# An attention, recurrence and feed-forward block with its attention rewritten on products of weights, in finer units woven into the recurrence

## What is computed

```
q, k, v = y @ Wq, y @ Wk, y @ Wv                       # 16 heads of 64
dots = q k^T * SCALE                                    # per sequence and head
pos  = (q . rel_emb[clip(i - j, -64, 64) + 64]) * SCALE
out  = softmax(dots + pos) @ v;  x = x + out @ Wo + bo
...
def step(h, xs):                                        # 256 times, in order
    z  = sigmoid(xzt + h @ U_z + vz)
    r  = sigmoid(xrt + h @ U_r + vr)
    hh = tanh(xht + r * h @ U + vh)
    return (1 - z) * h + z * hh
...
sel = argmax(h @ gate_w.T);  g = h w_gate[sel].T;  u = h w_up[sel].T   # scaled by sigmoid(top)
x = x + (u * silu(g)) @ w_down[sel].T
```

## Time and profile before

| | |
|---|---|
| median of 3 runs | 716.01 us (714.69 to 716.34) |
| span of the profiled execution, first to last instruction | 712.3 us |
| median less span | 3.7 us |
| PE busy | 623.2 us, 87% of the span |
| DVE, ACT, POOL busy | 461.2, 323.5, 177.9 us |
| keys, queries, values | 15.4 to 60.5 us |
| forty units ahead of the recurrence | to about 150 us |
| first and last `g` of the recurrence | 161.4 and 697.7 us |

### The profile page before, as it was taken

How to read it: one execution, slowest core, us unless ns; L and a number is a source line. 1 busy time by engine, 2 the same in 40 slices (tenths; PEclk the granted TensorE clock), 3 DMA queues, 4 the chain that set the end, 5 groups by cost and what they waited for, 6 DMA issues and landing times.

```text
span 712.3 us, 26221 instructions
## 1 busy us (share of the span) xinstructions
PE 623.2 (87%) x7909; PEld 511.6 (72%) x7909; DVE 461.2 (65%) x3362; ACT 323.5 (45%) x1253; POOL 177.9 (25%) x789
## 2 busy tenths in 40 slices
PE   5998888879888898989898989898888889999995
PEld 3445766658778777777787877777777677777864
DVE  1434666636777777777777777777766567766763
ACT  2355666623455555455555554555442223232221
POOL 1012444402332332333332323333211011111110
PEclk8999999977999999999999999999999999999996
DMA  8022555420222222222222222222210000000000
GB/s 231 3 82 59 145 154 140 132 67 25 74 74 69 66 66 66 66 71 71 68 70 68 66 66 66 67 75 66 74 25 2 2 2 6 7 5 4 5 8 6
DMA packets 47805, 43.08 MB, mean 60 GB/s; under 512 B 9340, under 2 KB 47496, under 8 KB 47624
## 3 DMA queue, kind: packets, MB, share of 16 engines
q1 hardware_dynamic: 47168, 40.76, 21.6%
q10 hardware_dynamic: 584, 1.64, 0.7%
HBM read 20.95 MB, written 21.43 MB: 59 GB/s over the span
## 4 chain that ended last, share of the span: by engine, by line
PE 59%; DVE 18%; issue 13%; ACT 7%; DMA 1%; DVEq 1%; SPq 1%; ACTq 0%; POOLq 0%; POOL 0%
PE bank L627 13%; PE bank L640 13%; PE bank L428 7%; PE bank L412 7%; DVE s_sb L850 4%; DVE o_sb L873 3%; ACT hh L770 3%; PE bank L445 2%; DVE g L1001 2%; DVE q L993 2%; ACT oT L656 2%; PE bank L460 2%; PE bank L532 2%; PE bank L462 2%; PE bank L458 2%
## 5 line engine op out<-in xcount | busy, mean ns | idle before, releaser
L360 POOL COPY x_nat<-d 128x4 f32 (+1 forms) x256 | 53.5, 209 | 391.8 <-DVE d L1006 391.8
L640 PE MATMUL bank<-q,uc 128*128 128x54 f32 (+1 forms) x512 | 106.2, 289 | 43.4 <-DVE q L993 41.0
L640 PEld LDWEIGHTS bank<-q,uc 128*128 128x128 f32 x512 | 77.7, 190 | 90.5 <-DVE q L993 85.8
L627 PE MATMUL bank<-g,uw 128*128 128x54 f16 (+1 forms) x2560 | 118.9, 189 | 3.6 <-DVE g L1001 3.6
L760 ACT ACTIVATE trz<-bank 128x8 f32<-128x8 f32 x256 | 45.5, 178 | 167.5 <-PE bank L627 167.2
L627 PEld LDWEIGHTS bank<-g,uw 128*128 128x128 bf16 x2560 | 103.3, 97 | 17.0 <-DVE g L1001 7.8
L627 PE MATMUL bank<-b,uw 128*128 128x54 f16 (+1 forms) x2560 | 110.1, 188 | 0.0
L627 PEld LDWEIGHTS bank<-b,uw 128*128 128x128 bf16 x2560 | 108.1, 103 | 1.1 <-issue 0.2
L770 ACT ACTIVATE hh<-bank 128x4 f32<-128x4 f32 x256 | 44.4, 174 | 135.6 <-PE bank L640 131.2
L1001 DVE TENSOR_TENSOR g<-z,hh 128x4 f16<-128x4 f32 x256 | 41.9, 164 | 97.4 <-ACT hh L770 97.4
L325 POOL COPY qa<-qT 64x64 f32 (+1 forms) x256 | 60.6, 237 | 102.3 <-PE bank L403 63.4
(11 more groups left out here) (133 smaller groups left out, 1025.4 us busy)
## 6 DMA issues: line engine op xcount, KB each, us to landing
skew<-e_sb SPq DMA_DIRECT2D x128, 159.5 KB, 2.2
pos<-skew SPq DMA_DIRECT2D x256, 64.0 KB, 2.4
...
out<-y_out SPq DMA_DIRECT2D x8, 64.0 KB
...
```

The lines of the kernel that those rows point to most:

```text
L627: ins = mm(out_, uw[:, gate, use, j, :], operand, start=False, stop=True, skip_group_check=True)
L640: mm(c_cols(k, n), uc[:, :], st["q8"][:, now, 0:n], start=False, stop=True, skip_group_check=True).then_inc(c_pre, 1)
```

## The change

**Attention by products of weights.** `q k^T` of a head is `y (Wq_h Wk_h^T) y^T`, since the width of `y` is 128. The new kernel computes the sixteen 128x128 products `Wq_h Wk_h^T` once (`m_sb`) and likewise `Wv_h Wo_h` (`vo_sb`). There are no keys and values: `scores` multiplies `gT = M y` by `yT`, `values` multiplies the weights by `y_nat`, and a product with `vo_sb` gives the head's part of the output directly. The queries `qT` remain, for the positions.

**Units of 32 tokens by 4 heads.** A unit (`unit`) is one sequence, 32 tokens and four heads, 128 rows; there are 16 in a chunk of 32 tokens and 128 in all, as before. Since the row is token by head, `gT` and `qT` serve as they are, and POOL copies nothing. The `q`, `g` and `o` products are 128x128 (`fill`), made for a whole chunk of four sequences; they go by the table `PERIOD` into 40 places of the 16 turns of a chunk, and DVE empties them, one call in an odd slot of a turn. DVE now divides the weights ahead of their transposes (`normalize`, L841, 128x256) and afterwards copies the output (`move_o`, L848). `positions` has 64 rows, `e_sb` gets narrower ends, SP issues one load in place of two. There is one PSUM bank each for positions, scores, and transposes with values.

**Where steps begin.** A turn of attention is one unit. The first step stands in turn 20 (`FIRST`), when the first chunk is done, and two steps go with each further turn. 222 steps lie beside attention, 34 behind it.

**The step.** The candidate and both gates have their own PSUM banks. `r` gets `g` by one fp32 product (L602), and `b` by five bf16 ones (L623, L626); `z` gets the whole state by one fp32 product (L605). All have four columns. ACT has `tr`, `tz` and `hh`; DVE has `q`, `b`, `b1`, `b2`, then its first slot of other work, then `g`, the new state straight into `hist`, and its second slot. POOL is not in the loop.

**Feed-forward last.** Seven tiles start in the 33 steps from step 223, the eighth after the last step; a tile has 9 steps in place of 14. SiLU is one activation from PSUM, scaled by the row's weight. Fillers stand only where PE's slot would be empty once attention is over. All loops are written out.

```diff
-PERIOD = 16
-BLOCK = PERIOD // 2
-EARLY = 5
-BEHIND = 3
-OVERLAP = GROUPS - EARLY
...
+CH = 32
+NCH = T // CH
+QUADS = 4
+UNITS = QUADS * B
...
+FIRST = 20
+SEED_TURN = 14
+LAST_TURN = N_UNITS + 3
+TILES = T // CH
+TOK = CH * B
+FFN_STEP = 2 * (LAST_TURN - FIRST) + 1
+TILE_STEPS = 9
...
+def unit(n):
+
+    c, k = divmod(n, UNITS)
+    quad, b = divmod(k, B)
+    return c, quad, quad // 2, quad % 2, b
+
+
+
+PERIOD = [("o", -1, 3), ("q", 1, 0), ("q", 1, 1), ("o", 0, 0), ("g", 1, 0), ("o", 0, 1), ("g", 1, 1), ("g", 1, 2),
+          ("o", 0, 2), ("g", 1, 3)]
+
+PLACES = [(k, s) for k in range(UNITS) for s in (("Be", "Ao") if k % 2 == 0 else ("Be", "Ao", "Bo"))]
...
+        r_bank, z_bank, c_bank, s_bank, to_bank, e_bank = bank[:6]
+        spare = bank[6:8]
...
+            pool.wait_ge(ld["gru"], 208)
+            pool.tensor_scalar(urg[:, :], wu[:, 0, :], 0.5, None, ALU.mult)
+            pool.tensor_scalar(uz[:, :], wu[:, 1, :], 0.5, None, ALU.mult)
+            pool.tensor_scalar(uc[:, :], wu[:, 2, :], 0.25, None, ALU.mult).then_inc(u_ok, 1)
...
+                if kind == "q":
+                    a = 4 * s + p
+                    ins = mm(to, wq_sb[:, a * 128:(a + 1) * 128], part, start=True, stop=True)
+                elif kind == "g":
+                    ins = mm(to, m_sb[:, s // 2, s % 2 * 4 + p, :], part, start=True, stop=True)
+                else:
+                    a = s % 2 * 4 + p
+                    ins = mm(fill_bank(j)[:, 0:128], vo_sb[:, s // 2, a, :],
+                             oT[:, c % 2, s // 2, a, :, :].rearrange("p b t -> p (b t)"), start=(p == 0), stop=(p == 3))
+                if p == 3:
+                    ins.then_inc(f_done, 1)
...
+                        ins = mm(bank[2 * s + e][:, k * 128:(k + 1) * 128], wqT[h, a, :], wkT[h, a, :], start=True, stop=True)
...
+            def transpose_p(n):
+                pe.wait_ge(pn_ready, n + 1)
+                if n >= 1:
+                    pe.wait_ge(o_ready, n)
...
+                    ins = mm(to_bank[:, T:T + 128], y_nat[:, 2 * b + r, :], pt_sb[:, n % 2, r * 128:(r + 1) * 128],
+                             start=(r == 0), stop=(r == 1))
+                ins.then_inc(o_done, 1)
...
+                        ins = mm(to[:, k * 128:(k + 1) * 128], wvT[h, 4 * s + k, :], wo_sb[h, 4 * s + k, :], start=True, stop=True)
...
+            def turn(n, slot):
+
+                if slot == "Ae" and 0 <= n < N_UNITS:
+                    scores(n)
+                if slot == "Be" and 0 <= n - 1 < N_UNITS:
+                    transpose_p(n - 1)
+                if slot == "Ao" and 0 <= n + LEAD < N_UNITS:
+                    positions(n + LEAD)
+                if slot == "Bo" and 0 <= n - 1 < N_UNITS:
+                    values(n - 1)
+                if (n, slot) in FILL_AT:
+                    fill(*FILL_AT[n, slot])
...
-            def period(i, groups, tiles, last):
...
-                    for use, name, ok in ((1, "b", (b1_ok, b2_ok)), (0, "g", (g1_ok, g2_ok))):
-                        if name == "g":
-                            first_window(i, k, groups, tiles, last)
-                        for low in range(2):
-                            pe.wait_ge(ok[low], t + 1)
-                            for gate in range(2):
-                                ins = product(rz_cols(k, gate, n), gate, use, st[f"{name}{low + 1}"][:, before, 0:n], low)
-                    ins.then_inc(rz_pre, 1)
-                    main_window(i, k, groups, tiles, last)
-                    pe.wait_ge(q8_ok, t + 1)
-                    mm(c_cols(k, n), uc[:, :], st["q8"][:, now, 0:n], start=False, stop=True, skip_group_check=True).then_inc(c_pre, 1)
...
+            for t in range(T):
+                n, odd = FIRST + t // 2, t % 2
+                now, before = t % 2, 1 - t % 2
+                if t >= 1:
+                    pe.wait_ge(g_ok, t)
+                    mm(r_bank[:, gate_cols(t)], urg[:, :], g_sb[:, before, :], start=False, stop=True,
+                       skip_group_check=True).then_inc(r_done, 1)
+                    pe.wait_ge(d_ok, t)
+                    mm(z_bank[:, gate_cols(t)], uz[:, :], hist[:, t, :], start=False, stop=True,
+                       skip_group_check=True).then_inc(z_done, 1)
+                if t % CH == 0:
+                    inputs(t // CH, 2)
+                turn(n, "Ao" if odd else "Ae")
+                tile_work(t, "A")
+                if n >= N_UNITS:
+                    fillers(t, "A")
+                pe.wait_ge(q_ok, t + 1)
+                mm(c_bank[:, gate_cols(t)], uc[:, :], q_sb[:, now, :], start=False, stop=True,
+                   skip_group_check=True).then_inc(c_done, 1)
+                if t + 1 < T:
+                    if (t + 1) % CH == 0:
+                        inputs((t + 1) // CH, 0)
+                    turn(n, "Bo" if odd else "Be")
+                    fillers(t, "B")
+                    pe.wait_ge(b1_ok, t + 1)
+                    for k in range(3):
+                        mm(r_bank[:, gate_cols(t + 1)], urb[:, k, :], b1[:, now, :], start=False, stop=True, skip_group_check=True)
+                    pe.wait_ge(b2_ok, t + 1)
+                    for k in range(2):
+                        mm(r_bank[:, gate_cols(t + 1)], urb[:, k, :], b2[:, now, :], start=False, stop=True, skip_group_check=True)
+                    if (t + 1) % CH == 0:
+                        inputs((t + 1) // CH, 1)
+                tile_work(t, "B")
...
+            for t in range(T):
+                n, odd = FIRST + t // 2, t % 2
+                now = t % 2
+                act.wait_ge(r_done, t + 1)
+                act.activation(tr[:, now, :], r_bank[:, gate_cols(t)], ACT.Tanh, scale=0.5).then_inc(tr_ok, 1)
+                again(t, 0)
+                act.wait_ge(z_done, t + 1)
+                act.activation(tz[:, now, :], z_bank[:, gate_cols(t)], ACT.Tanh, scale=0.5).then_inc(tz_ok, 1)
+                again(t, 1)
+                turn(n, "V1o" if odd else "V1e")
+                tile_work(t, "V1")
+                act.wait_ge(c_done, t + 1)
+                act.activation(hh[:, now, :], c_bank[:, gate_cols(t)], ACT.Tanh).then_inc(hh_ok, 1)
+                again(t, 2)
+                turn(n, "V2o" if odd else "V2e")
+                tile_work(t, "V2")
...
+            def turn(n, slot):
+                if slot == "W1e" and 0 <= n - 1 < N_UNITS:
+                    normalize(n - 1)
+                if slot == "W2e" and 0 <= n < N_UNITS:
+                    scores(n)
+                if slot == "W1o" and n in EMPTY_AT:
+                    emptied(*EMPTY_AT[n])
+                if slot == "W2o" and 0 <= n - 1 < N_UNITS:
+                    move_o(n - 1)
+                if slot == "W2o" and 0 <= n < N_UNITS:
+                    invert(n)
...
+            for t in range(T):
+                n, odd = FIRST + t // 2, t % 2
+                now = t % 2
+                state = hist[:, t, :]
+                if t >= 1:
+                    dve.wait_ge(d_ok, t)
+                else:
+                    dve.wait_ge(zeros_ok, 1)
+                dve.wait_ge(tr_ok, t + 1)
+                stt(q_sb[:, now, :], tr[:, now, :], 1.0, state, ALU.add, ALU.mult).then_inc(q_ok, 1)
+                dve.wait_ge(tz_ok, t + 1)
+                stt(b_sb[:, now, :], tz[:, now, :], -1.0, state, ALU.add, ALU.mult).then_inc(b_ok, 1)
+                if t + 1 < T:
+                    dve.wait_ge(b_ok, t + 1)
+                    dve.tensor_scalar(b1[:, now, :], b_sb[:, now, :], SPLIT, None, ALU.mult).then_inc(b1_ok, 1)
+                    dve.wait_ge(b1_ok, t + 1)
+                    stt(b2[:, now, :], b_sb[:, now, :], SPLIT, b1[:, now, :], ALU.mult, ALU.subtract).then_inc(b2_ok, 1)
+                turn(n, "W1o" if odd else "W1e")
+                tile_work(t, "W1")
+                dve.wait_ge(hh_ok, t + 1)
+                stt(g_sb[:, now, :], tz[:, now, :], 1.0, hh[:, now, :], ALU.add, ALU.mult).then_inc(g_ok, 1)
+                dve.wait_ge(g_ok, t + 1)
+                stt(hist[:, t + 1, :], b_sb[:, now, :], -0.5, g_sb[:, now, :], ALU.mult, ALU.add).then_inc(d_ok, 1)
+                turn(n, "W2o" if odd else "W2e")
+                tile_work(t, "W2")
```

1328 lines of the change are left out of this document (604 added, 724 removed).

## The result

The changed kernel takes 1,007.2 us (median of four runs, 1,002.9 to 1,011.5) beside 716.2 us of the kernel before in the same runs: a ratio of 1.409, 95% interval 1.402 to 1.417. The forecast was 669 us, its range 622 to 735. What came is rival C, and dearer than it was priced.

What follows compares the result with a forecast made beforehand. A chain repeated 256 times was taken to bound the kernel, with PE then waiting for DVE's division. 90 + 488.4 + 5.6 + 67.0 + 1.3 + 12.7 = 665.0 us of span, plus 3.7 around it: 669 us, range 622 to 735.

Steps and rivals of the forecast that it cites:

- rival C: PE's clock in the recurrence: granted 0.50, a step takes 3.15 us, all steps so 877 us; chance 0.13.
- those 1.87 us: PE's scores, transposes, positions, values and two and a half 128-column products per two steps, which double at the lower clock.
- the walk: Steps beside attention, operation by operation: even 2.37 us, PE waiting for DVE's division; odd 2.17; mean 2.27, taken as 2.21.
- tail: Span behind the last `g`: 12.7 us, bounds 11 and 15, in place of 14.6.
- first `g`: Start of the recurrence, behind nineteen turns of 2.4 us: 90 us, bounds 82 and 100, in place of 161.4.
- 221 steps beside attention with chunk ends: Recurrence beside attention: 221 steps of 2.21 us, 488.4, and seven new chunks at 0.8 us each, 5.6.
- 34 steps beside feed-forward with the table load: Last steps of the recurrence: 1.97 us each, 67.0 us, and one SiLU table load of 1.3 us.
- The 3.7 us around the span: Time outside the profiled span, added to 665.0 us of span to give the kernel's 669 us.
- rival B: Steps beside attention: a second stall adds 0.24 us, 2.45 us a step, 722 us in all; chance 0.15.
- Rival A: Steps beside attention: the division does not hold PE up, mean step 1.95 us, 611 us in all; chance 0.15.
- What would show it: Signs in the trace: PE's wait on `pn_sb` about 0.6 us, PEclk 1.00, 256-column matmuls above 0.6 us for rival C.
- part 1: The start, up to the first `g` at 90 us, 71 us gained; wrong if the first step came after 110 us.

Runs made afterwards that it cites:

- The last pair of kernels: Changed kernel with 54-column operands in all steps and products of zeros where the clock had fallen: 699.9 us, and 644.8 us with DVE dividing the weights right behind q_sb.
- the fastest kernel: Changed kernel with 54-column operands in all steps, products of zeros where the clock had fallen, and DVE's division of the weights right behind q_sb: 644.8 us.

## Why the prediction was wrong, point by point

**Rival C, the clock: the step that failed.** I saw the mechanism, priced all steps at 877 us, wrote that fifty of them would cancel the gain, and gave it 0.13. What outweighed it was "Against: two steps still carry those 1.87 us and eight to ten fp32 products". Those products are many instructions and little work: four columns each. In the earlier trace rows the products beside them are 54 columns wide, and I took the loss of that width for an edit without a cost. One line in the kernel before shows that the width was its clock: 876 us without it. The changed kernel with the width put back shows it from the other side: 734 us in place of 1,007. The wait for the division, which the walk had, took a share in it.

The Trainium skill, page "TensorE: Matmul & The Clock Gate", section "HAM oscillation", blames idle gaps between bursts; I wrote that by that rule C would not happen, and it did. As the whole cause the runs do not bear the gaps out: with the same wait of 0.36 us the clock fell within two steps at four columns and stood for most of the recurrence at 54, and at 0.50 PE was busy for 676.6 of 677 us without getting it back. As a part of it they do: without the wait the four-column kernel kept its clock to 208 us, and the profiles of the 54-column kernels have neither the fall near step 128 nor the one at 327 us. Behind the 1.29 us of idle PE at the table load the clock fell as well, and with six fillers in that gap it did not.

**Its price.** 3.15 us a step was forecast, 3.61 came beside attention (steps 16 to 192, 3.57 without a chunk end). I doubled the wide products and left the narrow ones as they were. From the start of one product to the next, the four-column fp32 product of `g` takes PE 0.42 us in place of 0.23, the state's 0.43 in place of 0.22, the candidate's 0.29 in place of 0.15 (the last of the rows at 0.50, L614 to L442): 0.54 more. The five bf16 products take 0.18 in place of 0.13. The wait for the division, 0.36 us in every second step, falls away: 0.18 less. 3.15 + 0.54 + 0.05 - 0.18 = 3.56. From step 192 on, where attention's products thin out, a step took 3.25 and then 2.92 us; the 221 steps with their chunk ends took 778.9 us in place of 701.8, 77 more. The 34 feed-forward steps took 108.3 us in place of 68.3, 40 more, where I had named 10 for the low level. With a start 10.7 us and a tail 1.0 us longer that is 129 us, the distance from 877 to 1,007.

**The sum with the clock up.** The last pair of kernels measures it, though with wide operands and fillers that the changed kernel lacks. The fastest run in the changed order took 692.0 us, 690.2 of span, at a mean clock of 0.998, but has no profile. The rows come from the profile of another run of that kernel, its steps at 0.50 replaced by like steps at 1.00 (an estimate), and for the 34 last steps from the fastest kernel. By my terms:

| term | forecast | measured at 1.00 |
|---|---|---|
| first `g` | 90 (82 to 100) | 99.7 |
| 221 steps beside attention with chunk ends | 494.0 | 503.4 |
| 34 steps beside feed-forward with the table load | 68.3 | 75.3 |
| tail | 12.7 | 11.7 |
| span | 665.0 | 690.1 |

So with the clock up the change is worth some 24 us, 3%, where I had 47; by the median of that kernel it is 16. "Faster" would have been right, the size half of it. The 3.7 us around the span were too many as well: they are a median less the span of another execution. Around one and the same execution lie 1.8 us in the changed kernel (1,003.4 and 1,001.6) and 2.2 in the kernel before (716.5 and 714.3).

*The start* was 0.7 us outside its bounds in the changed kernel, whose clock was at 0.50 for 3.4 us near 22 us; in the three kernels that kept the clock there the first `g` came at 96.5 to 99.7 us, inside them. Unit 0's scores were on DVE at 39.0 us, as forecast to the tenth, and that is luck in part: PE began on the queries 1.0 us later than my sum has it, the query products and products of weights took 6.9 us in place of 9.2, and the `g` fills 5.6 in place of 4.4. The turns were wrong, mostly 2.90 us in place of 2.40. One of them:

```profile
61.47 0.44 PE L442 MATMUL bank<-ident,pn_sb 128*128 128x128 f32 x2 [0.61 <-DVE pn_sb L841]
...
61.94 0.38 ACT L640 ACTIVATE pt_sb<-bank 128x256 f32<-128x256 f32 x1 [2.17 <-PE bank L442]
...
62.48 0.49 PE L398 MATMUL bank<-oT,vo_sb 128*128 128x128 f32 x2
...
62.80 0.61 PE L449 MATMUL bank<-pt_sb,y_nat 128*128 128x128 f32 x4
...
63.45 0.38 DVE L848 COPY oT<-bank 128x128 f32<-128x128 f32 x1 [1.16 <-PE bank L449]
```

The transposed weights are ready at 62.32, the values start at 62.80, because the positions and two products of the spare bank stand ahead of them on PE. My chain had them at once. Eighteen turns took 55.1 us from division to division, the longest 4.61, where I had 43.2 and 2 for delays: 9.9 of the 10.7 us. (Nineteen turns of 2.4 us are also 45.6 and not 45.2.) That putting them first does not help, the run on the order of the start showed.

*The step beside attention.* The walk gave 2.37 us for an even step and 2.17 for an odd one with a product of the spare bank. From L626 to L626, or its like, the even step took 2.35 and the odd one 2.06 or 2.28, by what it carries. The wait for the division was 0.36 to 0.44 us, not 0.6. Sixteen steps gave 2.27 without a chunk end, the 2.27 of the walk; the 0.06 that I took off for the shorter distances of the earlier trace rows was not there (13 us). A chunk end costs 1.0 us, not 0.8. The second stall of rival B was not there.

*Rival A* put the step without the stall at 1.95 us, from PE's list alone. With the early division two steps took 1.86 + 2.06 = 3.92 us, 1.96 each, or 2.03 over sixteen. The statement that PE waits for the division with everything behind it was right, and its removal was worth 0.245 us a step (2.303 to 2.058 over 192 steps), 47 us in all.

*The feed-forward steps* took 2.2 us at 1.00, not 1.97. The tile's products stand between those of the chain and are heavier than the two pairs per step that I counted; that this makes the difference no run tests.

**What would show it.** The wait on `pn_sb` came while the clock was up, smaller than 0.6. PEclk and the 256-column products, 1.20 us, spoke for C from the first look. The first step came 11 us late, short of the 110 us at which part 1 was to count as wrong.
